# Sixty-four experts on one core: groups in a pipeline, the second matrices held in the array, routing by group

## The reference

```
x = x + _L2_ffn_ref(_layernorm(x), ...)       # xf: 1600 tokens x 128
probs = softmax(xf @ router_w + router_b)     # 64 experts
tw, ti = top_k(probs, 8);  tw = tw / sum(tw)
for each expert e:  h = silu(xf @ W1 + B1) @ W2 + B2      # 128 -> 32 -> 128
                    acc = acc + (tw where ti == e) * h
shared = sum over 2 experts of silu(xf @ W1 + B1) @ W2 + B2   # 128 -> 256 -> 128
return acc + shared
```

## Time and profile before

| | |
|---|---|
| median of 3 runs | 2539.92 us (2537.13 to 2540.59) |
| profiled execution | 2547.37 us, its span 2545.6 us |
| PE busy, of the span | 84% |
| ACT busy, DVE busy | 57%, 51% |
| PE's mean granted clock | 0.916 |

### The profile page before, as it was taken

One profiled execution on the slowest core, in us unless ns is written; L12 is line 12 of the kernel. 1 busy time (PEld: TensorE's weight loads), 2 busy tenths in 40 slices (PEclk: granted clock), 3 DMA queues, 4 the chain that ended last, 5 costly groups with the idle time before them and its releaser, 6 DMA issues. The chain is left out here.

```text
span 2545.6 us, 45852 instructions
## 1 busy us (share of the span) xinstructions
PE 2148.0 (84%) x18128; PEld 1496.1 (59%) x18128; DVE 1288.3 (51%) x1666; ACT 1454.1 (57%) x1758; POOL 237.9 (9%) x305
## 2 busy tenths in 40 slices
PE   4767978979789469999748999979966999976998
PEld 2544855747558246666435666647744666655886
DVE  4552342334333566666557777743236666643111
ACT  2334445454454458888637888852235888872332
POOL 1005023140230400000010000010010000000000
PEclk9997989989889789999869999978987999996999
DMA  5758336354463568888046788620034887720000
GB/s 182 230 171 294 149 136 238 113 197 181 148 219 113 162 142 186 187 187 186 17 111 153 186 187 187 158 61 1 0 79 109 184 188 187 186 65 1 26 17 21
DMA packets 119703, 352.73 MB, mean 139 GB/s; under 512 B 20122, under 2 KB 54800, under 8 KB 118896
## 3 DMA queue, kind: packets, MB, share of 16 engines
q1 hardware_dynamic: 105728, 322.40, 46.6%
q0 software_dynamic: 13776, 27.54, 3.7%
HBM read 257.58 MB, written 91.23 MB: 137 GB/s over the span
## 5 line engine op out<-in xcount | busy, mean ns | idle before, releaser
L947 ACT ACTIVATE a_probs<-a_score 128x1200 f32<-128x1200 f32 x768 | 858.0, 1169 | 202.5 <-PE a_score L860 202.3
L860 PE MATMUL a_score<-a_qstack,a_kstack 128*128 128x400 f32 x2304 | 552.0, 371 | 56.9 <-DVE a_qstack L1030 56.0
L860 PEld LDWEIGHTS a_score<-a_qstack,a_kstack 128*128 128x128 f32 x2304 | 379.3, 190 | 227.3 <-issue 178.9
L822 PE MATMUL a_numer<-a_probs,a_v 128*18 128x200 f32 (+1 forms) x9216 | 470.2, 334 | 0.0
L822 PEld LDWEIGHTS a_numer<-a_probs,a_v 128*18 128x18 f32 (+1 forms) x9216 | 228.1, 97 | 183.7 <-issue 87.7
L1021 DVE TENSOR_TENSOR a_kstack<-a_kraw,a_kstack 64x2888 fp32r<-64x2888 f32 x90 | 284.8, 3165 | 2.8
L1030 DVE TENSOR_TENSOR a_qstack<-a_qrep,k_groupmask 128x1600 fp32r<-128x1600 f32 x48 | 87.6, 1826 | 172.3 <-PE a_score L860 143.1
L1016 DVE CAST a_kstack<-a_kraw 128x2888 fp32r<-128x2888 f32 x90 | 149.9, 1665 | 10.7 <-DVE a_own L1081 9.3
L1487 ACT ACTIVATE f3d_hidden<-f3d_ph,f_b 128x400 f32<-128x400 f32 x128 | 76.1, 594 | 117.3 <-PE f3d_ph L1445 110.0
L1697 PEld LDWEIGHTS f0r_ph<-f0r_xsT,f0r_w 128*128 128x128 f32 x896 | 118.8, 198 | 30.5 <-issue 12.5
L1697 PE MATMUL f0r_ph<-f0r_xsT,f0r_w 128*128 128x128 f32 x896 | 122.6, 281 | 9.3 <-DVE f0r_xsT L1878 9.3
(11 more groups left out here) (360 smaller groups left out, 2782.8 us busy)
## 6 DMA issues: line engine op xcount, KB each, us to landing
a_kraw<-keys SPq DMA_DIRECT2D x384, 361.0 KB, 6.2
values<-kv_vst SPq DMA_DIRECT2D x32, 1296.0 KB
a_v<-values SPq DMA_DIRECT2D x48, 864.0 KB, 5.8
keys<-kv_made SPq DMA_DIRECT2D x48, 722.0 KB
l0a_ctxT<-in_ctxT SPq DMA_DIRECT2D x16, 722.0 KB, 6.4
kv_ctxT<-in_ctxT SPq DMA_DIRECT2D x16, 722.0 KB, 6.6
l0a_ctx<-in_ctx SPq DMA_DIRECT2D x16, 704.0 KB
l0a_mask<-in_mask_BxSxS_ik SPq DMA_DIRECT2D x16, 564.1 KB
```

What stands on the lines that cost most here:

```text
L822: last = pe.matmul(numer[32 * g:32 * g + PC, p * 2 * SQ:(p + 1) * 2 * SQ], v[0:rows(t), j, t, (2 * g + p) * PC:(2 * g + p + 1) * PC], prob ...
L860: last = pe.matmul(to, kstack[:, j, g * SK + t * 128:g * SK + (t + 1) * 128], qstack[:, j, g * GH:(g + 1) * GH, :], start=True, stop=not s ...
L947: act.activation(probs[:, n % NP, :].rearrange("p (g q) -> p g q", g=SPAN), slot_ps[:, n % 2, :, 0:GQ], ACT.Exp, scale=HSCALE).then_inc(ex ...
```

## The change

- **Down.** The w2 chunk is held and `hidden`, 400 tokens, streams: one matmul for each of 20 chunks, and one with b2 for the bias. The sum comes out turned (features x tokens). ACT copies it to `yT` and adds the shared bias in passing (`keep_outputs`), PE turns it back in four transposes (`back`), and DVE adds it to x (`add`).
- **Pipeline.** PE issues in each of 20 slots an up of the next group, a pick and a down of this one. The shared chunks come first (`ORDER`), and a pick stands two slots ahead of its down. `hidden`, `own` and `yT` have two halves. `pw` has two banks in place of three.
- **Routing.** It is done group by group: that of group 0 ahead of all, that of group g+1 in three pieces between the scalings of group g (`softmax`, `choose`, `weigh`). There are two exponentials on ACT in place of one.
- **Ahead.** The router's loads have a semaphore of their own, and the ups of group 0 no longer wait for the exponential. The table `picked` and its copies are made by POOL during the layernorm.
- Loops are written out.

```diff
@@ l2_ffn
+    ORDER = tuple(range(HC2, CH)) + tuple(range(HC2))
...
+        def fills(pool):
             band = picked[:, :, :].rearrange("e c (j f) -> e (c j) f", f=H2)
             pool.memset(picked[:, :, :], 1.0).then_inc(cut, 1)
...
+            for part in range(2):
+                pool.dma_start(picker[part * E2:(part + 1) * E2, :, :].bitcast(F32), picked[:, :, :]).then_inc(picker_in, 16)
+        layernorm(nc, k, "ln2f", loads=loads, fills=fills)
...
+            def down(g, s):
+                ci = ORDER[s]
+                if s == 0 and g >= 2:
+                    pe.wait_ge(y_kept, g - 1)
+                if s == 0 and g == 1:
+                    pe.wait_ge(logits_kept, TG)
+                if s < SC2:
+                    pe.wait_ge(h_ready, g * CH + s + 1)
+                else:
+                    pe.wait_ge(scaled, g * HC2 + ci + 1)
+                pe.matmul(py[:, g % 2, 0:NTG], w2[:, ci, :], hidden[:, g % 2, s, :], start=(s == 0), stop=False)
...
+            pe.wait_ge(r_in, 32)
+            route(0)
+            pe.wait_ge(w_in, 128)
+            for s in range(CH):
+                up(0, s)
+                if s in (3, 7, 11):
+                    route((s + 1) // 4)
+                if s == 12:
+                    pe.matmul(pt[:, 0:2], sb2[:, :], k.ones[0:ES, 0:2], start=True, stop=True).then_inc(bias_full, 1)
+                if s == 13:
+                    turn(0)
+            pe.wait_ge(picker_in, 32)
+            for g in range(TG):
+                for s in range(CH):
+                    if g + 1 < TG:
+                        up(g + 1, s)
+                    if 2 <= s < CH - 2:
+                        pick(g, s - 2)
+                    down(g, s)
+                    if s == 3 and g:
+                        back(g - 1)
+                    if s == 15 and g + 1 < TG:
+                        turn(g + 1)
+                pe.matmul(py[:, g % 2, 0:NTG], b2[:, :], own[:, g % 2, :, :].bitcast(F32), start=False, stop=True).then_inc(y_full, 1)
+            back(TG - 1)
...
+            act.preload_act_table(ACT.Exp)
+            act.wait_ge(exp_ready, 1)
+            act.activation(e[:, 0:BG, :], e[:, 0:BG, :], ACT.Exp).then_inc(exped, 1)
+            act.preload_act_table(ACT.Silu)
+            for s in range(CH):
+                silu(0, s)
...
+            act.preload_act_table(ACT.Exp)
+            act.wait_ge(exp_ready, TG)
+            act.activation(e[:, BG:, :], e[:, BG:, :], ACT.Exp).then_inc(exped, 1)
+            act.preload_act_table(ACT.Silu)
+            for g in range(TG):
+                for s in range(CH):
+                    if g + 1 < TG:
+                        silu(g + 1, s)
+                    if s == 1 and g:
+                        keep_outputs(g - 1)
+                    if s == 15 and g + 1 < TG:
+                        keep_weights(g + 1)
+            keep_outputs(TG - 1)
...
+            for g in range(TG):
+                more = g + 1 < TG
                 for ci in range(HC2):
+                    scale(g, ci)
+                    if ci == 1 and more:
+                        softmax(g + 1)
+                    if ci == 3 and g:
+                        add(g - 1)
+                    if ci == 5 and more:
+                        choose(g + 1)
+                    if ci == 8 and more:
+                        weigh(g + 1)
+            add(TG - 1)
```

## The result

The change takes 2494.48 us (median of 4 runs, 2492.76 to 2497.96) where the kernel before took 2538.53 on the same chip (4 runs, 2537.02 to 2540.59): a ratio of 0.9828, 95% interval 0.9811 to 0.9845. Forecast were 2495.4 and a range of 2489 to 2506. The profiled execution of after took 2497.96, its span is 2496.2, the mean clock 0.916 as before.

A forecast was written before the change was run, and what follows sets the result against it. PE was taken as the stage's bound, by its own work and 2.4 us of gaps per group. Stage gain 45.3 less 0.8 for POOL gave 44.5, and 2539.92 - 44.5 = 2495.4 us; range 2489 to 2506.

The forecast's parts named there:

- The main sum: PE's stage, router to last addition: 20.1 + 0.6 + 30.8 + 63.2 + 17.9 + 2.7 = 135.3 us, 45.3 less than 180.6.
- the transposes: On PE: four new transposes as 8 records, 0.86 us, and the weights' transposes as 8 records, 0.43.
- The slot: Up, pick and down on PE in the looped groups: 0.667 + 0.187 + 0.667 = 1.52 us.
- the first case: The whole as summed: 2495.4 us, give or take clock 1.0, port 1.6 and runs' spread 2.8; chance 0.70.
- The rival of leaking slots: Ups stay coupled to silu at 0.775 us: 60 slots x 0.11 = 6.5 more, 2502; chance 0.13.
- DVE's pieces: Routing pieces of 1.9, 1.5 and 1.6 us fit in 2.0 and cost nothing; rival: 15 more, 2510, chance 0.05.
- The stall: PE waits once for a bank while ACT changes tables after the first 20 silus: 0.6 us.
- The clock: Rises some 5.5 us after the router starts; at 2.9, 1.0 less; never in the first ups, 12.8 more, chance 0.06.
- Nobody waits: During group 0's first ups silu can start 3.3 us after the router while PE makes three ups in 4.0.
- POOL under the layernorm: POOL's table making beside DVE's layernorm chain loses 0.8 us; bounds 0 and 2.4, one whole selection.
- the copies beside it: The picker's copies through POOL's queue at about 1690.5 land by 1698.7: cost nothing, at most 0.5 us.
- POOL is ready before the layernorm's barrier: At the layernorm's end, POOL's work was claimed finished before the barrier, so no cost was given.

The follow-up runs named there:

- kernel 4: The change with downs as before (hidden held, four matmuls of 128 columns, old bias products, nothing turned back): stage 156.5 against 133.9 us, median 2534.81.
- kernel 6: The change without DVE's routing of groups 1 to 3, which take group 0's weights: stage 133.8 against 133.9 us, median 2495.08.
- kernel 7: The change with ten more DVE reductions of 256 columns behind the first routing piece of each later group: stage 145.7 us, median 2506.62.
- kernel 1: The change with the table's two copies issued by SP behind the barrier, POOL still making it in the layernorm: ahead of router 15.4 against 16.9 us, median 2506.98.
- 5: The change with the next group's 20 ups put behind this group's downs, not interleaved, ACT's order fitted: stage 138.6 us, median 2499.95.
- kernel 9: As kernel 2, but POOL makes the table only after group 0's logits are handed to the exponential: stage 133.9 us, median 2504.82.
- kernel 10: As kernel 9, with attention's weight transfers behind the barrier and ACT's second cast of keys behind its query copies: median 2476.26, ratio to before 0.9700.
- the repeat: The unaltered change run again, on the chip of kernel 9 and kernel 10: stage 133.9 us, median 2512.14, ratio to before 0.9835.
- kernel 2: The change with POOL making the table behind the barrier and SP copying it: ahead of router 13.2, stage 135.2 us, median 2505.38.
- kernel 3: As kernel 2, with POOL's 16 output-matrix transfers behind the barrier in each of three attention stages: stage 138.4 us, median 2495.55.
- kernel 8: The change with one PE wait added, group 0's first up waiting for its exponential: stage 136.5 us, median 2496.86.

## Why the prediction was right, and where it was not

**The stage on PE.** Forecast 135.3, measured 133.9. The main sum held: router to the first up of group 1 took 20.1 (1694.69 to 1714.79), as summed. Group 0 with its stall took 31.6 (31.4 forecast), the next two 31.3 and 31.2 (31.6), the last 17.6 (17.9), the end 2.0 (2.7). The records behind it, the starts of groups 1 and 2 on PE:

```profile
1746.39 0.83 PE L1290 MATMUL f_ph<-k_xnT,f_w 128*128 128x400 f32 x2
...
1777.67 0.83 PE L1290 MATMUL f_ph<-k_xnT,f_w 128*128 128x400 f32 x2
```

What was too high is the transposes: I gave each two records, and they have one (so a matmul of f32 operands does not always stand as two).

```profile
L1332 PE MATMUL f_pt<-k_ident,f_yT 128*100 128x128 f32 x16 | 2.4, 275 | 0.7 <-ACT f_yT L1375 0.7
L1300 PE MATMUL f_pt<-k_ident,f_weights 100*128 100x100 f32 x16 | 2.0, 248 | 0.0
```

Sixteen transposes, sixteen records in each row. The trace of before had shown it: two groups' transposes, eight of them, stand there as eight records.

```profile
1721.95 0.85 PE L1364 MATMUL f_pw<-k_ident,f_weights 100*128 100x100 f32 x8
```

The end was shorter by the same and by quicker hand-overs: ACT's `yT` starts at 1826.55, the addition at 1827.88.

**The slot**, 1.52, held, and with it the first case; kernel 4 shows what the held operand is worth. The rival of leaking slots is out: behind the one stall below no wait on PE names silu. **DVE's pieces** cost nothing (kernel 6), and by kernel 7 the first of them, 1.7 long, could be 1.1 to 1.5 longer before PE waits: room for about 3 where the prediction had 2.0. **The stall** behind the tables cost 0.7, for 0.6: the up that waited starts at 1719.70 where the down ahead of it, at 1718.33, and 0.667 give 1719.00.

```profile
1719.06 2.22 ACT L1367 ACTIVATE f_hidden<-f_ph,f_b 128x400 f32<-128x400 f32 x4
1719.70 0.30 PEld L1290 LDWEIGHTS f_ph<-k_xnT,f_w 128*128 128x128 f32 x2 [1.18 <-ACT f_hidden L1367]
1719.70 0.94 PE L1290 MATMUL f_ph<-k_xnT,f_w 128*128 128x400 f32 x2 [0.54 <-ACT f_hidden L1367]
```

**The clock** rose 5.6 us after the router's first matmul, for the 5.5 taken. That was partly luck. PE's work up to there is the same in nearly all kernels, and the rise came after 3.6 (kernel 1), 3.7 (7), 4.3 (5), 5.3 to 5.9 (4, 6, 9, 10, the repeat), 6.2 (2) and 13.3 (3); in kernel 8, with its wait, after 8.7. The earlier place that I read as 2.9 is 3.1 (0.80 on the mean of a us in which it rises once). That an early rise gives 1.0 back did not hold: in kernel 1 it came 2.0 earlier, PE then waited 0.7 for silu, and the stage is 133.8. "Nobody waits" in the ramp was nearly so; one wait for silu of 0.96 stands on PE's loads at 1700.12.

**The step that was mis-sized is the one on POOL under the layernorm, and the copies beside it.** The sum had 0.8 for the first and nothing for the second; 3.8 was measured, in two parts.

*DVE was held for 2.2.* The first DVE instruction of the layernorm to the first L205 takes 8.08 before (1683.69 to 1691.77) and 10.25 after. The timeline of after:

```profile
1679.05 0.54 DVE L193 TENSOR_SCALAR ln2f_mean<-ln2f_total 100x8 f32<-100x8 f32 x1
1679.62 1.22 DVE L194 TENSOR_TENSOR ln2f_centred<-k_x,ln2f_mean 100x1024 f32<-100x1024 f32 x1
...
1682.01 1.08 DVE L193 TENSOR_SCALAR ln2f_mean<-ln2f_total 100x8 f32<-100x8 f32 x1
1683.13 1.22 DVE L194 TENSOR_TENSOR ln2f_centred<-k_x,ln2f_mean 100x1024 f32<-100x1024 f32 x1
...
1685.52 1.09 DVE L199 TENSOR_SCALAR ln2f_var<-ln2f_spread 100x8 f32<-100x8 f32 x1
```

and POOL's memset and selections there:

```profile
1677.76 1.80 POOL L1245 MEMSET f_picked<- 64x2048 f32 x1 [389.04 <-POOLq L88]
1679.63 6.94 POOL L1248 TENSOR_SCALAR_AFFINE_SELECT f_picked<-f_picked 64x2048 f32<-64x2048 f32 x2
```

The tiny `TENSOR_SCALAR` takes 0.17 in kernels 2 and 9; here it ends at 1679.59 where the memset ends at 1679.56, at 1683.09 where the first selection ends (1679.63 + 3.44 = 1683.07), and at 1686.61 where the second ends (1686.57). The wide subtractions keep their 1.22, and it is the selections that take 3.44 in place of 2.36, each 1.08 longer. So each side waits the other out in turn, with no semaphore between them. DVE's loss is 0.37 behind the memset, 0.91 behind the first selection and 0.92 behind the second: 2.2. I took 0.8 from 0.34 per us of casts, and had the rule beside it. The Trainium skill ("SBUF — State Buffer", Who interferes with whom) says that whoever has the shared ports keeps them for the whole instruction, that two inputs in SBUF contend with POOL's reads, and that `tensor_scalar` can contend too. The trace agrees with it in kind: each of the three waits lasts until POOL's instruction ends. That the sum, 2.2, also comes near the 2.4 that I had worked out by it, one whole selection waited out once, is chance; it is three waits, none of them whole. The row that I preferred, of short casts beside L205, misled. The 1.86 of kernel 2 agrees nearly: from 1703.08 it lasts until 1704.94, and the first selection there ends near 1704.7 (half of the row's 4.84).

*The barrier cost 1.6.* "POOL is ready before the layernorm's barrier" was the step: its last instruction was, its transfers weren't, and the barrier waited for them (kernels 1 and 3). In other kernels with the same step it cost up to 3.4 (kernel 7). That the copies were early enough for the first pick, as worked out, did not matter.

The two sizes, 3.0 too little ahead of the router and 1.4 too much behind it, came out 1.6 apart in the stage, inside the spread of the runs. That the median came within 1 us of the forecast is thus partly luck: two errors of opposite sign, and beside them differences of the program ahead that no term of the sum covers.

## What to carry to other kernels

When the next step's operand is wide and its stationary narrow, hold the full 128 columns, and let what is long stream; then put the next group's first products between this group's last ones, so that PE waits for nobody; here it was busy 31.00 of 31.00 us, and the clock stayed at 1.00. Look at what stands ahead of an end-of-block barrier on POOL: transfers that it has in flight hold all engines there, and moving 16 of them behind it, together with ACT's cast of the late keys (kernel 10), brought 24.6 us in three stages here, over half of what the change itself brought. The transfers alone brought 10.8 (kernel 3 against 2). Work moved onto POOL "in the shadow" can hold DVE until POOL's instruction ends; place it where DVE's chain has slack, as in kernel 9, where 3.0 us of such waits cost nothing.

## What the runs showed of the hardware

- A barrier behind a block in which POOL issued transfers opened 2.3 us behind the last compute instruction (2.25 to 4.06 in the other kernels that do so), and 0.7 where SP issued them later; in the attention stages of before ACT stood 8.3 to 10.0 there, and 0.7 in the first of them in kernel 10. SP's transfers in flight did not hold it (kernel 3).
- A `TENSOR_SCALAR` of 8 columns took 1.08 in place of 0.17 beside a POOL selection, and a selection 3.44 in place of 2.36 beside DVE's subtraction of 1024 columns. In kernel 9 a `TENSOR_TENSOR` of 256 columns took 2.51 in place of 0.43 beside a selection, which kept its time.
- PE's loads of 128 columns (0.19 each) lie wholly beside the matmuls: PE is busy 31.00 of 31.00 us with 19.0 of loads.
- The granted clock rose from 0.50 to full 5.6 us after the router's first matmul in the change, 3.6 after it in kernel 1 and 13.3 in kernel 3. Kernel 2, with the same wait of 1.2 us as kernel 3, took 6.2: no run here shows what decides it.
